# Cross-attention: value products of all four head groups in one place, partial sums in places of their own

## The chip, the cores and the metric

The kernel runs on one core of a Trainium2 chip. The metric is the device time of one execution in microseconds. The engines are TensorE (PE, with its weight loads as PEld), VectorE (DVE), ScalarE (ACT), GpSimd (POOL) and SyncE (SP), which only issues DMAs here.

## What is computed

One decoder layer on x (32 batches of 112 tokens, 512 wide): causal self-attention, cross-attention to a context of 375 tokens for each batch, and a quantised feed-forward part, each with a residual and a layer norm. The change is in the cross-attention, cut here to what matters:

```
q, k, v = hs @ Wq.T + bq, ctx @ Wk.T + bk, ctx @ Wv.T + bv     # 16 heads of 32
s      = clip(q k^T / sqrt(32), -50, 50), masked to -10000, clipped again
p      = softmax(s)                                            # over 375 tokens
ctx    = p v ; delta = rs * (ctx @ Wo.T + bo)
delta  = layernorm(delta) * gamma + beta
x      = layernorm(x + delta)
```

## The kernel before

`self_attention`, `cross_attention` and `ffn` follow each other. In `cross_attention` each engine has its own hand-written program, a loop over 32 batches b, tied to the others by semaphores. The order of the work on an engine is the order in which its `body(b, par, pair)` calls its helpers.

The 16 heads are four groups h of four heads, and the 375 context tokens are three thirds t of 125. Scores, with tokens on partitions, are 125 x 4 x 112 for one (h, t); the twelve of a batch are made in three **score blocks** of four (`score_pieces`, which splits them by group and third). Per batch:

- **TensorE** (`body`, L1293 and on): `scores` (L1286) of block 0; `attend_pair` of the batch before for head groups 2 and 3, that is two `attend` (value products, L1260, 12 matmuls each) and `sums` (L1267, column sums of the probabilities); `keys` 2 (L1206), `values` 2 (L1217); scores of block 1; keys 3; `output` of the batch before (L1238, one 128-row tile of x, into the bank `bKV[1]`); scores of block 2; `attend_pair` of this batch for groups 0 and 1; then keys 0, values 0, keys 1, values 1 of the next batch. keys write `bKV[0]`, values and output write `bKV[1]`, so each waits until the product before it in that bank was read.
- **ScalarE**: `probabilities` (L976, the exponentials of a block into `pr[h]`), copies of keys (L950) and values (L956), and `split_high` (L944), the cast of the raw context of batch b+2.
- **VectorE** (L1158 and on): `limits(b, 0)` (L1156, four instructions a block, clipping and masking), `attended(b-1, 1)`, `split_low(b+1)` (L1008, the low part of the next context, after which its raw buffer `craw` may be loaded again), `limits(b, 1)`, `tail1` (bias and statistics of the output; its first instruction, L1113, reads `bKV[1]`), `limits(b, 2)`, `attended(b, 0)`, `tail2` and `tail3` (residual, norm, row maxima). `attended(b, p)` normalises one pair of groups: a reciprocal of the sums (L1046), a product (L1048), the high parts (L1030) and low parts (L1036) into the output's operand `cT`. `cT` holds 256 columns, so 12 of the 32 batches wrap round in it and need two pieces, which doubles the instructions of L1030 and L1036.
- **GpSimd**: for each group two adds over the thirds, L920 into `psum01` and L924 into `psum`, so that `sums` has one product in place of three; between them `x1_beta` (L904) and two reciprocal roots (L908, L912). An add for a group waits until its three thirds are through `limits`.
- **SP** loads `craw` for batch b+2 (L872) once `split_low(b+1)` is done, the queries of b+1 and the x tile, and stores results.

`tile_of(b)` maps a batch to its output tile; for b = 0, 8, 16, 24 there is none, since 8 batches make 7 tiles. So the batches 1, 9, 17 and 25 have no output product and no tail; `third_value(b)` gives them another order, keys 2 ahead of the attend_pair and values 2 behind keys 3. They are called short batches, the other 26 between batch 1 and batch 31 common ones. `values` for t == 0 waits (`dl_ok`) until tail1's L1113 has read the bank:

```
if t == 0:
    wait(pe, clo_ok, b)
    wait(pe, dl_ok, tiles_done(b - 2))
```

Of the kernel before, what the change touches and what calls it, by code (L numbers as in the profile page):

```python
# [9 lines left out]
ALU = mybir.AluOpType  # L10
# [4 lines left out]
B, S, D = 32, 112, 512  # L15
T = 375
TP = 376
P = 128
C = D // P
# [731 lines left out]
def cross_attention(nc, ctxT, maskT, craw, w, bk, bv, bo, ln_gamma, ln_beta, rscale, x1_d, q_d, x2_d, x2_first, amax):  # L751
# [6 lines left out]
    with ExitStack() as ctx:  # L758
# [5 lines left out]
        bot, gam, bet = n.sb("bo", [P, D]), n.sb("gam", [P, D]), n.sb("bet", [P, D])  # L764
# [12 lines left out]
        psum01, psum = n.sb("psum01", [TW, NJ, S]), n.sb("psum", [TW, NJ, 2 * S])  # L777
        spare = LEFT["qb"][:].rearrange("p b c s -> p (b c s)")
        one, at, rinv = spare[0:1, D:D + P], spare[:, D + P:D + P + 2 * S], spare[:, D + P + 2 * S:D + P + 4 * S]
        CR = 2  # L780
# [66 lines left out]
        def _(sp):  # L847
# [15 lines left out]
            for t, src in ((bot, row(bo, P)), (gam, row(ln_gamma, P)), (bet, row(ln_beta, P))):  # L863
                sp.dma_start(t[:], src).then_inc(small_in, 16)
            sp.wait_ge(x1_out, 16 * NG)
            sp.dma_start(wraw_o[:], xwo).then_inc(wo_in, 16)
            sp.wait_ge(q_out, 16 * (NG + 1))

# [20 lines left out]
        def _(pool):  # L889
# [10 lines left out]
            def x1_beta(t):  # L900
# [3 lines left out]
                nc.gpsimd.tensor_tensor(x1[t % 2][:], x1[t % 2][:], bet[:], ALU.add).then_inc(x1b_ok, 1)  # L904
# [9 lines left out]
            def body(b, par, pair):  # L914
                tail = tile_of(b - 1)
                for h in range(C):
                    if not (last(b) and h >= 2):
                        pool.wait_ge(pr_ok, 12 * b + 3 * h + 3)
                        wait(pool, ps_ok, 4 * b + h)
                        nc.gpsimd.tensor_tensor(psum01[:], third(h, 0), third(h, 1), ALU.add).then_inc(p01_ok, 1)  # L920
                        pool.wait_ge(p01_ok, 4 * b + h + 1)
                        if h % 2 == 0:
                            wait(pool, sum_done, 2 * b + h // 2)
                        nc.gpsimd.tensor_tensor(psum[:, :, value_columns(h)], psum01[:], third(h, 2), ALU.add).then_inc(ps_ok, 1)  # L924
# [80 lines left out]
        def _(dve):  # L1005
# [152 lines left out]
            def body(b, par, pair):  # L1158
                tail = tile_of(b - 1)
                limits(b, 0)  # L1160
                if not first(b):
                    attended(b - 1, 1)
# [12 lines left out]
                attended(b, 0)  # L1175
# [25 lines left out]
        def _(pe):  # L1201
            def keys(b, par, m):
                wait(pe, k_ok, 4 * b + m)
                for c in range(C):
# [59 lines left out]
            def sums(b, p):  # L1264
                pe.wait_ge(ps_ok, 4 * b + 2 * p + 2)
                for j in range(NJ):
                    mm = nc.tensor.matmul(bPV[p][j * HD:(j + 1) * HD, 2 * S:4 * S], ones[0:TW, :], psum[:, j, :], start=True, stop=True)  # L1267
# [22 lines left out]
            def attend_pair(b, par, p):  # L1290
                for h in (2 * p, 2 * p + 1):
                    attend(b, par, h)
                sums(b, p)  # L1293

            def body(b, par, pair):
# [3 lines left out]
                if not first(b):  # L1299
                    attend_pair(b - 1, 1 - par, 1)  # L1300
# [10 lines left out]
                attend_pair(b, par, 0)  # L1311
                if not last(b):
# [534 lines left out]
```

## Time and profile before

| | |
|---|---|
| three runs | 1435.27, 1436.67, 1438.06 us; median 1436.67 |
| the profiled execution | 1435.54 us, its span 1433.7 us |
| busy, share of the span | PE 98%, PEld 78%, DVE 75%, ACT 48%, POOL 38% |
| POOL L920, 126 adds | 166.2 us, 1319 ns each; idle before them 288.0 us, waiting for DVE L1156 |
| DVE L1156, 384 limits | 221.6 us, 635 ns each |
| DVE L1046, 63 reciprocals | 97.5 us, 1548 ns each |
| PE L1260, 3072 records | 87.6 us |
| PE L1267, 504 records | 35.4 us |
| ctxT into wraw, 32 loads | 752 KB each, 4.9 us to landing |

The cross-attention runs from about 355 to 1213 us of the span. Busy time alone does not bound it: a matmul's record contains its drain, which the next one overlaps, so the distance between starts is what a stage costs TensorE. Idle time of an engine counts only where another waits for what it then does. In the profile's timelines a row merges neighbours of one kind: start, length, engine, line, operands, count, and in brackets the idle time before it and what ended that.

### The profile page before, as it was taken

The numbers are of one execution on the slowest core, as the hardware profiler recorded it, in microseconds if no ns is written. First come the engines' busy times: TensorE is split into PE (matmuls) and PEld (weight loads), VectorE is DVE, ScalarE is ACT, GpSimd is POOL, SyncE is SP. The second block draws the span as 40 slices with busy tenths as digits, with TensorE's granted clock in tenths as the row PEclk, the third lists the DMA queues.
The fourth block names the chain that finished last, engine by engine and source line by source line (L and its number), as shares of the span: only waits on it lengthen the run. The fifth ranks groups of instructions, "written<-read, shape, count | busy, mean of one in ns | idle before, by whom it ended". The sixth has DMA issues, their size and how long they took to land. (4 is left out here: it accounts for less than half of the span.)

```text
span 1433.7 us, 30674 instructions
## 1 busy us (share of the span) xinstructions
PE 1400.7 (98%) x12827; PEld 1116.9 (78%) x12836; DVE 1080.2 (75%) x2010; ACT 685.9 (48%) x995; POOL 545.1 (38%) x499
## 2 busy tenths in 40 slices
PE   8999999999999999999999999999999996999998
PEld 4889898987888888888888888888888885555443
DVE  5888676654568878777787778878768877677898
ACT  2444444442443343443343434434433434888996
POOL 1000000000345444454554444544444542752676
PEclk9999999999999999999999999999999998999999
DMA  6536424232321121121211211211212121338896
GB/s 227 166 100 166 141 97 134 101 113 104 109 73 44 51 80 43 45 72 52 66 57 51 72 37 51 80 47 50 71 45 79 44 63 48 104 134 321 279 342 208
DMA packets 93882, 149.34 MB, mean 104 GB/s; under 512 B 14002, under 2 KB 61746, under 8 KB 91954
## 3 DMA queue, kind: packets, MB, share of 16 engines
q1 hardware_dynamic: 93746, 147.41, 31.3%
q8 instruction: 100, 1.64, 0.5%
q14 instruction: 36, 0.29, 0.1%
HBM read 101.25 MB, written 44.04 MB: 101 GB/s over the span
## 5 line engine op out<-in xcount | busy, mean ns | idle before, releaser
L1156 DVE TENSOR_SCALAR xa_pr<-xa_pr,xa_keep 125x448 f32<-125x448 f32 x384 | 221.6, 635 | 92.0 <-ACT xa_pr L976 91.4
L920 POOL TENSOR_TENSOR xa_psum<-xa_pr 125x448 f32<-125x448 f32 x126 | 166.2, 1319 | 288.0 <-DVE xa_pr L1156 287.0
L976 ACT ACTIVATE xa_pr<-xa_bSC 125x1344 f32<-125x1344 f32 (+2 forms) x192 | 165.7, 916 | 131.2 <-PE xa_bSC L1286 131.2
L956 ACT COPY xa_v<-xa_bKV 125x512 f32<-125x512 f32 x96 | 56.3, 587 | 215.1 <-PE xa_bKV L1217 209.6
L924 POOL TENSOR_TENSOR xa_psum<-xa_psum,xa_pr 125x448 f32<-125x448 f32 x126 | 147.7, 1172 | 10.2 <-PE xa_bPV L1267 0.7
L1206 PE MATMUL xa_bKV<-left_xn,wA 128*128 128x376 f32 x768 | 148.3, 341 | 0.0
L1206 PE MATMUL xa_bKV<-xa_cx,wA 128*128 128x376 f32 x768 | 147.5, 341 | 0.0
L950 ACT ACTIVATE xa_kf<-xa_bKV,xa_bk 128x376 f32<-128x376 f32 x128 | 73.7, 576 | 150.2 <-PE xa_bKV L1206 150.0
L1217 PE MATMUL xa_bKV<-wZ,left_xn 128*125 128x512 f32 x576 | 141.8, 394 | 1.9 <-POOL xa_ones L891 1.9
L1206 PEld LDWEIGHTS xa_bKV<-left_xn,wA 128*128 128x128 f32 x768 | 131.2, 188 | 14.2 <-issue 10.7
L1206 PEld LDWEIGHTS xa_bKV<-xa_cx,wA 128*128 128x128 f32 x768 | 130.2, 188 | 13.7 <-issue 10.0
L1217 PE MATMUL xa_bKV<-wZ,xa_cx 128*125 128x512 f32 x576 | 140.8, 393 | 0.0
L1217 PEld LDWEIGHTS xa_bKV<-wZ,left_xn 128*125 128x125 f32 x576 | 106.0, 185 | 25.2 <-POOL xa_ones L891 2.3
L1217 PEld LDWEIGHTS xa_bKV<-wZ,xa_cx 128*125 128x125 f32 x576 | 106.0, 185 | 21.8
L1286 PEld LDWEIGHTS xa_bSC<-xa_qf,xa_kf 32*125 32x125 f32 x3072 | 92.4, 183 | 36.4 <-issue 35.4
L1286 PE MATMUL xa_bSC<-xa_qf,xa_kf 32*125 32x112 f32 x3072 | 109.4, 279 | 1.4 <-ACT xa_kf L950 1.4
L1766 PE MATMUL ff_bF<-w2q,ff_hq 128*128 128x512 bf16 x439 | 98.1, 384 | 3.6 <-DVE ff_hq L1664 2.1
L1046 DVE RECIPROCAL left_qb<-xa_bPV 128x224 f32<-128x224 f32 x63 | 97.5, 1548 | 4.2 <-PE xa_bPV L1267 4.2
L1743 PE MATMUL ff_bF<-ff_xqT,w1q 128*128 128x448 bf16 x512 | 99.9, 357 | 0.2 <-DVE ff_xqT L1640 0.2
L1766 PEld LDWEIGHTS ff_bF<-w2q,ff_hq 128*128 128x128 bf16 x448 | 44.1, 99 | 57.3 <-issue 4.9
L1260 PE MATMUL xa_bPV<-xa_pr,xa_v 125*32 125x112 f32 x3072 | 87.6, 262 | 0.4 <-DVE xa_pr L1156 0.4
L1743 PEld LDWEIGHTS ff_bF<-ff_xqT,w1q 128*128 128x128 bf16 x512 | 50.1, 99 | 47.0 <-issue 1.7
(252 smaller groups left out, 2413.5 us busy)
## 6 DMA issues: line engine op xcount, KB each, us to landing
wraw<-in_ctxT SPq DMA_DIRECT2D x32, 752.0 KB, 4.9
ff_hr<-h_scratch SPq DMA_DIRECT2D x28, 512.0 KB, 6.3
wraw<-in_w SPq DMA_DIRECT2D x7, 1024.0 KB, 5.1
xa_qf<-q_scratch SPq DMA_DIRECT2D x32, 224.0 KB, 4.9
xa_x<-x_scratch SPq DMA_DIRECT2D x28, 256.0 KB, 4.9
x_scratch<-xa_x SPq DMA_DIRECT2D x28, 256.0 KB, 2.0
h_scratch<-ff_hq SPq DMA_DIRECT2D x8, 896.0 KB, 4.9
h_scratch<-ff_hs SPq DMA_DIRECT2D x8, 896.0 KB, 4.4
```

Source lines behind the costliest of these rows:

```text
L920: nc.gpsimd.tensor_tensor(psum01[:], third(h, 0), third(h, 1), ALU.add).then_inc(p01_ok, 1)
L924: nc.gpsimd.tensor_tensor(psum[:, :, value_columns(h)], psum01[:], third(h, 2), ALU.add).then_inc(ps_ok, 1)
L950: nc.scalar.activation(kf[:, m, :], bKV[0][:, 0:TP], ACT.Identity, bias=bkt[:, m:m + 1]).then_inc(k_ok, 1)
L976: nc.scalar.activation(pr[h][:, :, t * S:(t + size) * S], bSC[0:TW, :, slot * S:(slot + size) * S], ACT.Exp, scale=XSCALE).then_inc(exp_ok, 1)
L1046: nc.vector.reciprocal(rinv, bank[:, 2 * S:4 * S]).then_inc(ri_ok, 1)
L1156: nc.vector.tensor_scalar(third(h, t), third(h, t), EM50, keep[:, b * TC + t:b * TC + t + 1], ALU.max, ALU.min).then_inc(pr_ok, 1)
L1206: mm = nc.tensor.matmul(bKV[0][:, 0:TP], w["k"][l][:, c, m * P:(m + 1) * P], cx[par][r][:, c, :], start=c == 0 and k == 0, stop=c == C - 1 ...
L1217: mm = nc.tensor.matmul(bKV[1][0:TW, 0:D], cx[par][l][:, c, t * TW:(t + 1) * TW], w["v"][r][:, c, :], start=c == 0 and k == 0, stop=c == C ...
L1260: mm = nc.tensor.matmul(bank[j * HD:(j + 1) * HD, value_columns(h)], v[par][:, t, h * P + j * HD:h * P + (j + 1) * HD], pr[h][:, j, t * S: ...
L1286: mm = nc.tensor.matmul(bSC[0:TW, j, i * S:(i + 1) * S], kf[own, h, t * TW:(t + 1) * TW], qf[par][own, h, :], start=True, stop=True)
L1743: mm = nc.tensor.matmul(bF[m % 4][:, 0:GT], w1q[:, c, m * P:(m + 1) * P], xqT[par][:, c, :], start=c == 0, stop=c == C - 1)
L1766: mm = nc.tensor.matmul(bF[(UT * u + j) % 8][:, 0:D], hq[:, u % 2, m, j * P:(j + 1) * P], w2q[:, m, :], start=m == 0, stop=m == M - 1)
```

## The change

`attend_pairs` replaces `attend_pair`: behind score block 0 of batch b TensorE now makes the value products of all four head groups of batch b-1 and then both sum groups. None are left behind score block 2, but in the last batch, whose first two groups stay there. VectorE's `attended(b-1, 0)` and `attended(b-1, 1)` both come first in its batch. GpSimd's partial sums of a batch have four places of their own in a `psum` twice as wide; `psum01` goes, the second add is made in place, and the first waits for the sums of the batch before. `bet` (ln_beta) moves into a spare part of another buffer to make room, so it is loaded later. `keys` for m == 0 waits for `clo_ok` itself.

```
-        bot, gam, bet = n.sb("bo", [P, D]), n.sb("gam", [P, D]), n.sb("bet", [P, D])
+        bot, gam = n.sb("bo", [P, D]), n.sb("gam", [P, D])
...
-        psum01, psum = n.sb("psum01", [TW, NJ, S]), n.sb("psum", [TW, NJ, 2 * S])
+        psum = n.sb("psum", [TW, NJ, C * S])
...
+        bet = spare[:, D + P + 4 * S:2 * D + P + 4 * S]
...
             sp.wait_ge(q_out, 16 * (NG + 1))
+            sp.dma_start(bet, row(ln_beta, P)).then_inc(small_in, 16)
...
                         pool.wait_ge(pr_ok, 12 * b + 3 * h + 3)
-                        wait(pool, ps_ok, 4 * b + h)
-                        nc.gpsimd.tensor_tensor(psum01[:], third(h, 0), third(h, 1), ALU.add).then_inc(p01_ok, 1)
+                        own = psum[:, :, h * S:(h + 1) * S]
+                        wait(pool, sum_done, 2 * b + h // 2 - 1)
+                        nc.gpsimd.tensor_tensor(own, third(h, 0), third(h, 1), ALU.add).then_inc(p01_ok, 1)
                         pool.wait_ge(p01_ok, 4 * b + h + 1)
-                        if h % 2 == 0:
-                            wait(pool, sum_done, 2 * b + h // 2)
-                        nc.gpsimd.tensor_tensor(psum[:, :, value_columns(h)], psum01[:], third(h, 2), ALU.add).then_inc(ps_ok, 1)
+                        nc.gpsimd.tensor_tensor(own, own, third(h, 2), ALU.add).then_inc(ps_ok, 1)
...
                 tail = tile_of(b - 1)
+                if not first(b):
+                    attended(b - 1, 0)
+                    attended(b - 1, 1)
                 limits(b, 0)
-                if not first(b):
-                    attended(b - 1, 1)
...
-                attended(b, 0)
+                if last(b):
+                    attended(b, 0)
...
                 wait(pe, k_ok, 4 * b + m)
+                if m == 0:
+                    wait(pe, clo_ok, b)
...
-            def attend_pair(b, par, p):
-                for h in (2 * p, 2 * p + 1):
-                    attend(b, par, h)
-                sums(b, p)
+            def attend_pairs(b, par, pairs):
+                for p in pairs:
+                    attend(b, par, 2 * p)
+                    attend(b, par, 2 * p + 1)
+                for p in pairs:
+                    sums(b, p)
...
                 if not first(b):
-                    attend_pair(b - 1, 1 - par, 1)
+                    attend_pairs(b - 1, 1 - par, range(2))
...
                 scores(b, par, 2)
-                attend_pair(b, par, 0)
-                if not last(b):
+                if last(b):
+                    attend_pairs(b, par, range(1))
+                else:
                     for t in range(2):
                         keys(b + 1, 1 - par, t)
                         values(b + 1, 1 - par, t)
```

TensorE, one common batch, from its first score block (L1286, after the change L1291) to the next batch's keys. `xa_bSC` are scores, `xa_bPV` value products and sums, `xa_bKV` keys, values and output. Before:

```order
L1286 MATMUL xa_bSC<-xa_qf,xa_kf 125x112 x16
L1260 MATMUL xa_bPV<-xa_pr,xa_v 32x112 x24
L1267 MATMUL xa_bPV<-xa_psum,xa_ones 32x224 x4
L1206 MATMUL xa_bKV<-xa_cx,wA 128x376 x12
L1217 MATMUL xa_bKV<-wZ,xa_cx 125x512 x12
L1286 MATMUL xa_bSC<-xa_qf,xa_kf 125x112 x16
L1206 MATMUL xa_bKV<-xa_cx,wA 128x376 x12
L1238 MATMUL xa_bKV<-wQ,xa_cT 128x512 x12
L1286 MATMUL xa_bSC<-xa_qf,xa_kf 125x112 x16
L1260 MATMUL xa_bPV<-xa_pr,xa_v 32x112 x24
L1267 MATMUL xa_bPV<-xa_psum,xa_ones 32x224 x4
L1206 MATMUL xa_bKV<-left_xn,wA 128x376 x12
```

and after the change:

```order
L1291 MATMUL xa_bSC<-xa_qf,xa_kf 125x112 x16
L1265 MATMUL xa_bPV<-xa_pr,xa_v 32x112 x48
L1272 MATMUL xa_bPV<-xa_psum,xa_ones 32x224 x8
L1211 MATMUL xa_bKV<-xa_cx,wA 128x376 x12
L1222 MATMUL xa_bKV<-wZ,xa_cx 125x512 x12
L1291 MATMUL xa_bSC<-xa_qf,xa_kf 125x112 x16
L1211 MATMUL xa_bKV<-xa_cx,wA 128x376 x12
L1243 MATMUL xa_bKV<-wQ,xa_cT 128x512 x12
L1291 MATMUL xa_bSC<-xa_qf,xa_kf 125x112 x16
L1211 MATMUL xa_bKV<-left_xn,wA 128x376 x12
```

The rows of 24 value products and 4 sums behind the third score block are gone, and those behind the first have doubled.

VectorE, one common batch in which the batch before is not cut in pieces, from its first instruction behind the tail before to the first of tail1 (L1113, then L1114). `left_qb` holds the reciprocals and products, `xa_cT` is the output's operand. Before:

```order
L1156 TENSOR_SCALAR xa_pr<-xa_pr,xa_keep 125x4x112 x4
L1046 RECIPROCAL left_qb<-xa_bPV 128x224
L1048 TENSOR_TENSOR left_qb<-xa_bPV,left_qb 128x224
L1030 TENSOR_SCALAR xa_cT<-left_qb,xa_bv 128x112 x2
L1036 SCALAR_TENSOR_TENSOR xa_cT<-left_qb,xa_bv,xa_cT 128x112 x2
L1008 TENSOR_TENSOR xa_cx<-wraw,xa_cx 128x1504
L1156 TENSOR_SCALAR xa_pr<-xa_pr,xa_keep 125x4x112 x4
L1113 TENSOR_TENSOR left_qb<-xa_bKV,xa_bo 128x512
```

and after the change:

```order
L1047 RECIPROCAL left_qb<-xa_bPV 128x224
L1049 TENSOR_TENSOR left_qb<-xa_bPV,left_qb 128x224
L1031 TENSOR_SCALAR xa_cT<-left_qb,xa_bv 128x112 x2
L1037 SCALAR_TENSOR_TENSOR xa_cT<-left_qb,xa_bv,xa_cT 128x112 x2
L1047 RECIPROCAL left_qb<-xa_bPV 128x224
L1049 TENSOR_TENSOR left_qb<-xa_bPV,left_qb 128x224
L1031 TENSOR_SCALAR xa_cT<-left_qb,xa_bv 128x112 x2
L1037 SCALAR_TENSOR_TENSOR xa_cT<-left_qb,xa_bv,xa_cT 128x112 x2
L1157 TENSOR_SCALAR xa_pr<-xa_pr,xa_keep 125x4x112 x4
L1009 TENSOR_TENSOR xa_cx<-wraw,xa_cx 128x1504
L1157 TENSOR_SCALAR xa_pr<-xa_pr,xa_keep 125x4x112 x4
L1114 TENSOR_TENSOR left_qb<-xa_bKV,xa_bo 128x512
```

A second reciprocal with its product and parts has come in, and both now stand ahead of the first four limits, and so ahead of L1008 (L1009), split_low, and of all that follows it.

## Rows read from the trace of the kernel before

**Rows 1.** Timeline, PE, one common batch (start us, us, engine, line, operation, count)

```profile
702.98 1.14 PE L1286 MATMUL xa_bSC<-xa_qf,xa_kf 32*125 32x112 f32 x32
704.04 1.36 PE L1260 MATMUL xa_bPV<-xa_pr,xa_v 125*32 125x112 f32 x48
...
717.90 1.36 PE L1260 MATMUL xa_bPV<-xa_pr,xa_v 125*32 125x112 f32 x48
719.07 0.56 PE L1267 MATMUL xa_bPV<-xa_psum,xa_ones 125*32 125x224 f32 x8
719.56 2.35 PE L1206 MATMUL xa_bKV<-left_xn,wA 128*128 128x376 f32 x12
721.75 2.96 PE L1217 MATMUL xa_bKV<-wZ,left_xn 128*125 128x512 f32 x12
...
729.49 1.14 PE L1286 MATMUL xa_bSC<-xa_qf,xa_kf 32*125 32x112 f32 x32
```

**Rows 2.** Timeline, PE, batch 1, a short one

```profile
389.86 1.14 PE L1286 MATMUL xa_bSC<-xa_qf,xa_kf 32*125 32x112 f32 x32
...
393.18 1.36 PE L1260 MATMUL xa_bPV<-xa_pr,xa_v 125*32 125x112 f32 x48
...
403.84 2.35 PE L1206 MATMUL xa_bKV<-left_xn,wA 128*128 128x376 f32 x12
...
413.77 1.14 PE L1286 MATMUL xa_bSC<-xa_qf,xa_kf 32*125 32x112 f32 x32
```

**Rows 3.** Timeline, DVE, normalising a pair: whole, then parts of one in pieces

```profile
394.99 1.56 DVE L1046 RECIPROCAL left_qb<-xa_bPV 128x224 f32<-128x224 f32 x1 [1.05 <-PE xa_bPV L1267]
...
397.01 0.47 DVE L1030 TENSOR_SCALAR xa_cT<-left_qb,xa_bv 128x112 fp32r<-128x112 f32 x2
...
397.88 1.72 DVE L1008 TENSOR_TENSOR left_xn<-wraw,left_xn 128x1504 fp32r<-128x1504 f32 x1
...
724.86 0.99 DVE L1030 TENSOR_SCALAR xa_cT<-left_qb,xa_bv 128x80 fp32r<-128x80 f32 x4
...
725.77 0.83 DVE L1036 SCALAR_TENSOR_TENSOR xa_cT<-left_qb,xa_bv,xa_cT 128x80 fp32r<-128x80 f32 x4
```

**Rows 4.** Timeline, DVE and POOL, limits, split_low and adds, batch 0 and a common one

```profile
369.55 1.54 DVE L1156 TENSOR_SCALAR xa_pr<-xa_pr,xa_keep 125x448 f32<-125x448 f32 x4 [7.91 <-ACT xa_pr L976]
...
370.81 2.91 POOL L920 TENSOR_TENSOR xa_psum<-xa_pr 125x448 f32<-125x448 f32 x1 [10.94 <-DVE xa_pr L1156]
371.01 1.72 DVE L1008 TENSOR_TENSOR xa_cx<-wraw,xa_cx 128x1504 fp32r<-128x1504 f32 x1
...
711.03 1.71 DVE L1008 TENSOR_TENSOR left_xn<-wraw,left_xn 128x1504 fp32r<-128x1504 f32 x1
...
716.94 0.69 DVE L1113 TENSOR_TENSOR left_qb<-xa_bKV,xa_bo 128x512 f32<-128x512 f32 x1 [1.51 <-PE xa_bKV L1238]
...
719.51 3.34 DVE L1156 TENSOR_SCALAR xa_pr<-xa_pr,xa_keep 125x448 f32<-125x448 f32 x4
...
720.03 1.30 POOL L920 TENSOR_TENSOR xa_psum<-xa_pr 125x448 f32<-125x448 f32 x1
```

**Rows 5.** Groups of instructions by line (busy us, mean ns of one, idle before)

```profile
L924 POOL TENSOR_TENSOR xa_psum<-xa_psum,xa_pr 125x448 f32<-125x448 f32 x126 | 147.7, 1172 | 10.2 <-PE xa_bPV L1267 0.7
...
L950 ACT ACTIVATE xa_kf<-xa_bKV,xa_bk 128x376 f32<-128x376 f32 x128 | 73.7, 576 | 150.2 <-PE xa_bKV L1206 150.0
...
L904 POOL TENSOR_TENSOR xa_x<-xa_x,xa_bet 128x512 f32<-128x512 f32 x28 | 36.2, 1293 | 0.0
```

**Rows 6.** Timeline, SP's queue and ACT, batch 1: the raw context and its cast

```profile
399.62 0.55 SPq L872 DMA_DIRECT2D wraw<-in_ctxT  x1
...
404.52 1.45 ACT L944 CAST xa_cx<-wraw 128x1504 fp32r<-128x1504 f32 x1 [0.65 <-DMA wraw<-in_ctxT]
```

**Rows 7.** Timeline, PE, last batch, value products of group 2

```profile
1191.95 0.78 PE L1260 MATMUL xa_bPV<-xa_pr,xa_v 125*32 125x112 f32 x24 [0.38 <-DVE xa_pr L1156]
```

**Rows 8.** Stretches: us, PE, PEld, DVE, ACT, POOL busy, PEclk, DMA share, GB/s

```profile
1198.00:1199.00 1.00, 1.00 (x11) 0.43 (x13) 0.74 (x3) 0.00 (x0) 0.00 (x0) 0.57 0.00 0
```

More of the change, by code:

```diff
@@ L862, in _ @@
             sp.dma_start(craw, ctxT[1]).then_inc(c_in, 16)
-            for t, src in ((bot, row(bo, P)), (gam, row(ln_gamma, P)), (bet, row(ln_beta, P))):
+            for t, src in ((bot, row(bo, P)), (gam, row(ln_gamma, P))):
                 sp.dma_start(t[:], src).then_inc(small_in, 16)
@@ L903, in x1_beta @@
                 pool.wait_ge(x1_in[t % 2], 16 * (t // 2) + 16)
-                nc.gpsimd.tensor_tensor(x1[t % 2][:], x1[t % 2][:], bet[:], ALU.add).then_inc(x1b_ok, 1)
+                nc.gpsimd.tensor_tensor(x1[t % 2][:], x1[t % 2][:], bet, ALU.add).then_inc(x1b_ok, 1)
             def norm(t):
@@ L1266, in sums @@
                 for j in range(NJ):
-                    mm = nc.tensor.matmul(bPV[p][j * HD:(j + 1) * HD, 2 * S:4 * S], ones[0:TW, :], psum[:, j, :], start=True, stop=True)
+                    mm = nc.tensor.matmul(bPV[p][j * HD:(j + 1) * HD, 2 * S:4 * S], ones[0:TW, :], psum[:, j, 2 * p * S:2 * (p + 1) * S], start=True, stop=True)
                 mm.then_inc(sum_done, 1)
```

## The prediction

> **What bounds the kernel now.** I read the table of waits first: from batch 1 on TensorE hardly waits in the whole stage, so I went to its order of time and looked at one batch as a sum of stages. In [rows 1] a common batch runs from its first score block at 702.98 to the next at 729.49, 26.51 us, with each stage beginning where the last one ends. The other kind, batches 1, 9, 17 and 25, has no output product; batch 1 takes from 389.86 to 413.77, 23.91 us [rows 2]. Of the 31 steps from one batch to the next, 26 are common, 4 are short, and one is batch 0's. So TensorE is the bound in this stage, and VectorE, ScalarE and GpSimd run behind it. Then I read VectorE's order of time beside GpSimd's, since the change reorders VectorE's work. VectorE is busy for most of a batch, so it has no large reserve, and what matters is which of its results TensorE waits for, and when.
>
> **What TensorE saves.** The value products and sums behind score block 2 go. In [rows 1] they hold TensorE from 717.90 to 719.56, 1.66 us. In the first place 24 value products and 4 sums are added to equal ones. Products run from 717.90 to 719.07, 1.17 us for 24 with the change of shape; the added 24 I put at 1.10. A sum group holds 0.49 (719.07 to 719.56); the added one at 0.38, near the 0.35 of the shortest possible overlap of its two passes (the group's own record is 0.56 long, most of it drain). Both ends: 1.45 and 1.66. So TensorE gains 0.18 a batch, between 0 and 0.21. That is all the change can give there: at most 31 x 0.18 = 5.6 us. Batch 0 has no pair from before it, so it loses the whole 1.66.
>
> **What VectorE now delays.** Times below count from the start of a batch's first score block. Formerly VectorE began a batch with the limits of block 0, normalised one pair behind them (the second pair of the batch before), and the other pair at the batch's end, behind all limits. Now both pairs of the batch before come first. They can't begin until the sums are there: score block 1.06 (702.98 to 704.04), the extra products 1.10, and from the first product to the reciprocal 1.81 (393.18 to 394.99) [rows 1 to 3]: 3.97. One pair takes 2.89 (394.99 to 397.88) [rows 3], two take 5.78, to 9.75. Limits of block 0: 1.46 (369.55 to 371.01) [rows 4], to **11.2**. Only then comes split_low, which began at 8.05 before (711.03 - 702.98); there follow the limits of block 1 and tail1, whose first instruction frees the bank in which TensorE puts the next batch's first value product.
>
> Limits and GpSimd's sums get in each other's way. Four limits take 1.54 alone and 3.34 when two adds run beside them, and the add that began at 370.81, just before split_low, took 2.91, while split_low took its usual 1.72 [rows 4]. So the two engines exclude each other, instruction by instruction. In the changed order GpSimd gets the first head's probabilities at 11, and its two adds, x1_beta and the next head's first add all fall on the limits of block 1, where formerly the first two had already run beside the reciprocal. With L920 1.30 [rows 4], L924 1.17 and L904 1.29 [rows 5]: split_low 1.72; the blocked add ends 2.71 behind split_low's start (371.01 to 373.72); then 1.17 + 1.29 + 1.30, small gaps of 0.1, and 0.25 for the last limit: 6.8 from 11.2, so **18.0**. The read of the output bank (L1113) adds 0.69 [rows 4]: 18.7, 18.75 with the signal.
>
> The Trainium skill (SBUF — State Buffer, "Who interferes with whom") says that a VectorE instruction with two SBUF inputs and a reading GpSimd instruction exclude each other and that issue order decides who blocks. By that rule split_low, issued 0.2 behind the add, would wait for it, about 0.9 us that the row of batch 0 does not show; the sum below would be 3.6 us longer, over four short batches.
>
> **Common batches.** TensorE could begin the value product at 721.75 - 702.98 - 0.18 = 18.6. It waits for 18.75 and, its weights no longer loaded ahead, loses 0.1 more; from there 7.74 (721.75 to 729.49) [rows 1]: 26.6. Against 26.51 that is **+0.1**. In 12 of the 26 the batch before is cut into two pieces by the 256-column buffer, and each pair has eight small instructions in place of four: 0.99 + 0.83 [rows 3] against 0.47 and the rest to 397.88, 0.87 together. The difference is at most 0.95, but the first of the four had to wait for an add. I take 0.5 a pair: **+1.1** a batch (bounds +0.6 and +1.9).
>
> **Short batches.** TensorE's products begin at 3.32 (389.86 to 393.18) [rows 2], so VectorE is 2.26 later: split_low begins at 13.5 and is done at 15.2. TensorE reaches the next batch's keys at 403.84 - 389.86 = 13.98, less 0.17 (a wait for a sum that goes), less 0.18: 13.6. It waits **1.6**. split_low also frees the raw context for its transfer: 4.90 from issue to the cast (399.62 to 404.52), cast 1.45 [rows 6], the copy of the keys 0.58 [rows 5]: 22.2, where TensorE wants the second key product at 15.2 + 4.97 = 20.2 (one keys and one values product, half of 719.56 to 729.49 [rows 1]). It waits **2.0** more. Then 4.97 to the end: 27.2 against 23.91, **+3.3**, four times. In common batches the transfer lands at 11.2 + 1.7 + 4.9 = 17.8, and score block 2 ends only at 16.4 (717.90 - 702.98 + 1.48), with its exponentials ahead of the cast: nothing.
>
> **The end.** In the last batch TensorE waits for the limits of block 2 already, 0.38 [rows 7]. They start at 16.53 in a common batch (719.51 - 702.98); now at 11.2 + 5.2 (limits of block 1 with the same four GpSimd instructions, without split_low) + 2.57 of tail1 (716.94 to 719.51) = 19.0 [rows 4]. I take **+2.3**, between 1.5 and 3. The load of ln_beta moves on SP's queue behind the waits for x1_out and q_out, ahead of the first wait for split_low; it is first used in batch 2, so nothing. GpSimd's own adds keep their number and size (in place and strided: the second add was strided before, and 1.17), nothing.
>
> **Sum.** 14 x 0.1 + 12 x 1.1 + 4 x 3.3 - 1.7 + 2.3 = 1.4 + 13.2 + 13.2 + 0.6 = **+28.4**. The profiled execution took 1435.5 us around a span of 1433.7; that gives 1463.9. The median of the three runs is 1.1 above it: **1465**.
>
> **Rivals.** (A) Limits and adds interleave better than I have it: VectorE passes its four limits of block 1 before GpSimd's second add, so they end near 11.2 + 1.7 + 1.5 = 14.4 and tail1's read waits only for the output product, as before. For it speaks 369.55 to 371.01, four limits and split_low without a delay, against it 3.34 for four. Then common batches gain 0.18 and only the short ones and the ends lose: -4.7 + 13.2 + 0.6 = +9, **1446**. (B) They interleave worse, or a pair costs 3.4 (the split ones 4): a microsecond more in each of 26 batches, **1491**; for it speaks that the order of the two engines is a matter of tenths. (C) The clock. After TensorE's pause at the end of the stage the granted clock fell from 1.0 to 0.5, 0.57 in the microsecond at 1198 [rows 8], which is 1.2 in place of 2.4 GHz; the pause before it was 2.5 us. If each short batch's two pauses (1.6 and 2.0) did the same for 3.4 us, 1.7 us lost each time, it is 7 to 14 more: **1475**. (D) On the other side, faster: VectorE's chain is short enough everywhere, TensorE keeps its 0.18 in all batches and the short ones don't wait: -5.6 and -1.7, **1430**. It needs split_low done by 13.6 in the short batches, so pairs of at most 2.1 us, where a reciprocal alone is 1.56 [rows 3] and the product and four other instructions follow; and a transfer of under 3 us. I see no room for it.
>
> **How the numbers follow.** Forecast 0.56, A 0.16, B 0.12, C 0.11, D 0.05. The forecast's own bounds are 1457 to 1479 (the cut batches 7 to 23 in place of 13, the short ones 12 to 17, the end 1.5 to 3). The range takes in A and C and leaves out B and D: **1445 to 1485**. About 0.2% (2.9 us) is what a measurement here tells from no change. Faster 0.04, within it 0.02, slower 0.94.
>
> **What would show it.** Right: TensorE waits at its values line for VectorE's L1114 in common batches, about 0.2 and 1.3 us by turns, at the keys line for split_low and for ScalarE's key copy in batches 1, 9, 17 and 25, near 2 us each; score blocks 26.6 and 27.6 apart by turns, and 27.2 in the short ones; reciprocals start 4.0 behind the batch. Wrong: waits of TensorE only in the short batches (A), or over 2 us in common ones (B), a granted clock of 0.5 within the stage (C), batches 26.3 apart (D).

## The result, and the profile after

The changed kernel takes **1472.53 us**, the median of four runs (1471.5 to 1477.62), against 1436.18 for the kernel before on the same chip: a ratio of **1.0258, 95% interval 1.0246 to 1.027** (here and below estimated from the single runs, so not quite the quotient of the two medians). It is slower by 36 us. The profiled execution took 1471.5 us around a span of 1469.7, 36.0 more than the 1433.7 of before, so its trace can be read against the sum of the prediction as it stands.

The page's groups for the limits (L1157), the first and the second add of a head (L923, L925), and from the view by lines the add of ln_beta to x1 (L906):

```profile
L923 POOL TENSOR_TENSOR xa_psum<-xa_pr 125x448 f32<-125x448 f32 x126 | 210.0, 1667 | 378.3 <-DVE xa_pr L1157 377.4
L1157 DVE TENSOR_SCALAR xa_pr<-xa_pr,xa_keep 125x448 f32<-125x448 f32 x384 | 319.6, 894 | 10.6 <-ACT xa_pr L977 10.5
...
L925 POOL TENSOR_TENSOR xa_psum<-xa_psum,xa_pr 125x448 f32<-125x448 f32 x126 | 157.1, 1247 | 9.9
...
L906 POOL TENSOR_TENSOR xa_x<-xa_x,left_qb 128x512 f32<-128x512 f32 x28 | 40.0, 1427 | 0.0
```

The same 384 limits, on the same data, took 98 us more than before (319.6 against 221.6, that is 384 x 635 ns, on the page of before). The adds are longer too: the first took 1319 ns before, the second 1172 ns [rows 5]. No work was added to either engine; they stand in each other's way more often. What TensorE makes of it stands in its table of waits (total in us, times, longest):

```profile
PE xa_bKV L1222 <- DVE left_qb L1114: 15.5, 17, 1.5
PE xa_bKV L1211 <- DVE left_xn L1009: 6.8, 4, 1.7
PE xa_bKV L1211 <- ACT xa_kf L951: 6.4, 4, 2.3
```

None of the three was there before. The first is the read of the output bank, in common batches; the other two are split_low and the key copy, once each in the four short batches. Here is TensorE's order of time in one common batch whose pairs are cut in pieces:

```profile
741.78 1.14 PE L1291 MATMUL xa_bSC<-xa_qf,xa_kf 32*125 32x112 f32 x32
742.85 2.51 PE L1265 MATMUL xa_bPV<-xa_pr,xa_v 125*32 125x112 f32 x96
745.17 0.94 PE L1272 MATMUL xa_bPV<-xa_psum,xa_ones 125*32 125x224 f32 x16
746.04 2.35 PE L1211 MATMUL xa_bKV<-left_xn,wA 128*128 128x376 f32 x12
...
758.29 2.32 PE L1211 MATMUL xa_bKV<-xa_cx,wA 128*128 128x376 f32 x12
761.77 3.02 PE L1222 MATMUL xa_bKV<-wZ,xa_cx 128*125 128x512 f32 x12 [1.16 <-DVE left_qb L1114]
...
769.56 0.70 PE L1291 MATMUL xa_bSC<-xa_qf,xa_kf 32*125 32x112 f32 x16
```

and VectorE's and GpSimd's in the same batch:

```profile
745.80 1.56 DVE L1047 RECIPROCAL left_qb<-xa_bPV 128x224 f32<-128x224 f32 x1 [1.82 <-PE xa_bPV L1272]
...
749.28 1.55 DVE L1047 RECIPROCAL left_qb<-xa_bPV 128x224 f32<-128x224 f32 x1
...
752.68 1.54 DVE L1157 TENSOR_SCALAR xa_pr<-xa_pr,xa_keep 125x448 f32<-125x448 f32 x4
754.13 1.72 DVE L1009 TENSOR_TENSOR xa_cx<-wraw,xa_cx 128x1504 fp32r<-128x1504 f32 x1
755.77 5.26 DVE L1157 TENSOR_SCALAR xa_pr<-xa_pr,xa_keep 125x448 f32<-125x448 f32 x4
760.95 0.68 DVE L1114 TENSOR_TENSOR left_qb<-xa_bKV,xa_bo 128x512 f32<-128x512 f32 x1
...
753.93 2.93 POOL L923 TENSOR_TENSOR xa_psum<-xa_pr 125x448 f32<-125x448 f32 x1 [11.25 <-DVE xa_pr L1157]
756.95 1.17 POOL L925 TENSOR_TENSOR xa_psum<-xa_psum,xa_pr 125x448 f32<-125x448 f32 x1
758.07 1.44 POOL L906 TENSOR_TENSOR xa_x<-xa_x,left_qb 128x512 f32<-128x512 f32 x1
759.47 1.31 POOL L923 TENSOR_TENSOR xa_psum<-xa_pr 125x448 f32<-125x448 f32 x1
```

Read it as a chain. Value products for all four head groups and their sums stand between the score block and the next keys, which follow 4.26 us behind its start; the reciprocal begins at 4.02. Two pairs, in pieces here, take 3.48 and 3.40. Then come the limits of block 0, split_low, and four limits that take 5.26 us in place of 1.54, because each has one of GpSimd's four adds in its way. (GpSimd's first, L923, is the one that had begun before split_low.) L1114, which frees the output bank, starts 19.17 behind the batch. TensorE stood ready at 760.6 and waits 1.16 us. In the kernel before, the same read waited 1.51 us for TensorE, not the other way round [rows 4].

The two waits of a short batch, batch 1, by VectorE, TensorE and ScalarE:

```profile
401.31 1.72 DVE L1009 TENSOR_TENSOR left_xn<-wraw,left_xn 128x1504 fp32r<-128x1504 f32 x1
...
403.18 2.32 PE L1211 MATMUL xa_bKV<-left_xn,wA 128*128 128x376 f32 x12 [1.69 <-DVE left_xn L1009]
...
407.80 1.45 ACT L945 CAST xa_cx<-wraw 128x1504 fp32r<-128x1504 f32 x1 [4.51 <-DMA wraw<-in_ctxT]
409.15 0.57 ACT L951 ACTIVATE xa_kf<-xa_bKV,xa_bk 128x376 f32<-128x376 f32 x1
...
409.77 2.33 PE L1211 MATMUL xa_bKV<-left_xn,wA 128*128 128x376 f32 x12 [1.48 <-ACT xa_kf L951]
...
414.81 1.14 PE L1291 MATMUL xa_bSC<-xa_qf,xa_kf 32*125 32x112 f32 x32
```

Distances from score block to score block, read from TensorE's order of time over the whole stage, for both kernels and the eight experiments (us):

| kernel | batch 0 | short (1, 9, 17, 25) | common, not cut / cut | first to last score block |
|---|---|---|---|---|
| before | 22.83 | 23.91, 23.91, 23.75, 23.75 | 26.51 to 26.54 / the same | 807.89 |
| changed | 21.16 | 27.08, 27.07, 28.33, 27.92 | 26.70 to 26.79 / 27.79 to 28.13 | 840.26 |
| places alone | 22.84 | 23.89 to 23.91 | 26.51 to 26.54 / the same | 808.20 |
| VectorE's order alone | 22.84 | 29.46, 29.40, 26.78, 28.31 | 26.51 to 26.54 / the same | 826.53 |
| split_low first | 21.18 | 23.61 | 26.36 to 26.39 / the same | 801.47 |
| ln_beta's add later | 21.18 | 27.25, 27.22, 28.13, 28.01 | 26.36 to 26.39 / 26.75 to 27.13 | 822.81 |
| split_low first in short batches | 21.16 | 23.61 | 26.70 to 26.79 / 27.79 to 28.14 | 824.47 |
| limits and split_low first | 21.17 | 23.61 | 27.36 to 27.59 / 28.43 to 30.05 | 853.08 |
| split_low first, last batch | 21.17 | 23.61 | 26.36 to 26.39 / the same | 801.46 |
| before, split_low first | 22.83 | 23.75 | 26.51 to 26.54 / the same | 807.56 |

### The profile page after: what moved, and what is told of

The parts are those of the page before. It is cut to its first block and busy times, and to the rows that moved or that the text cites. A ratio compares the mean times of both kernels' runs of the same rounds, so it can differ in the third digit from the quotient of the medians.

```text
span 1469.7 us, 30639 instructions
## 1 busy us (share of the span) xinstructions
PE 1404.3 (96%) x12827; PEld 1118.9 (76%) x12836; DVE 1161.1 (79%) x2010; ACT 683.4 (46%) x995; POOL 599.0 (41%) x499
## 5 line engine op out<-in xcount | busy, mean ns | idle before, releaser
L923 POOL TENSOR_TENSOR xa_psum<-xa_pr 125x448 f32<-125x448 f32 x126 | 210.0, 1667 | 378.3 <-DVE xa_pr L1157 377.4
L1157 DVE TENSOR_SCALAR xa_pr<-xa_pr,xa_keep 125x448 f32<-125x448 f32 x384 | 319.6, 894 | 10.6 <-ACT xa_pr L977 10.5
L1211 PE MATMUL xa_bKV<-left_xn,wA 128*128 128x376 f32 x768 | 150.1, 344 | 13.2 <-DVE left_xn L1009 6.8
L925 POOL TENSOR_TENSOR xa_psum<-xa_psum,xa_pr 125x448 f32<-125x448 f32 x126 | 157.1, 1247 | 9.9
L1222 PE MATMUL xa_bKV<-wZ,left_xn 128*125 128x512 f32 x576 | 142.7, 396 | 10.7 <-DVE left_qb L1114 8.4
L1222 PE MATMUL xa_bKV<-wZ,xa_cx 128*125 128x512 f32 x576 | 142.2, 395 | 8.2 <-DVE left_qb L1114 7.0
L1222 PEld LDWEIGHTS xa_bKV<-wZ,left_xn 128*125 128x125 f32 x576 | 105.3, 185 | 37.2 <-issue 11.6
L1222 PEld LDWEIGHTS xa_bKV<-wZ,xa_cx 128*125 128x125 f32 x576 | 105.1, 185 | 34.4 <-issue 12.4
L1291 PEld LDWEIGHTS xa_bSC<-xa_qf,xa_kf 32*125 32x125 f32 x3072 | 92.4, 183 | 36.4 <-issue 34.0
L1291 PE MATMUL xa_bSC<-xa_qf,xa_kf 32*125 32x112 f32 x3072 | 109.5, 279 | 1.4 <-ACT xa_kf L951 1.4
L1243 PE MATMUL xa_bKV<-wQ,xa_cT 128*128 128x512 f32 x336 | 83.9, 398 | 3.6 <-DVE xa_cT L1037 3.6
```

Of the source, the lines that this page charges most:

```text
L923: nc.gpsimd.tensor_tensor(own, third(h, 0), third(h, 1), ALU.add).then_inc(p01_ok, 1)
L925: nc.gpsimd.tensor_tensor(own, own, third(h, 2), ALU.add).then_inc(ps_ok, 1)
L1157: nc.vector.tensor_scalar(third(h, t), third(h, t), EM50, keep[:, b * TC + t:b * TC + t + 1], ALU.max, ALU.min).then_inc(pr_ok, 1)
L1211: mm = nc.tensor.matmul(bKV[0][:, 0:TP], w["k"][l][:, c, m * P:(m + 1) * P], cx[par][r][:, c, :], start=c == 0 and k == 0, stop=c == C - 1 ...
L1222: mm = nc.tensor.matmul(bKV[1][0:TW, 0:D], cx[par][l][:, c, t * TW:(t + 1) * TW], w["v"][r][:, c, :], start=c == 0 and k == 0, stop=c == C ...
L1243: mm = nc.tensor.matmul(bKV[1][:, 0:D], cT[l][:, c, own], w["o"][r][:, c, :], start=c == 0 and k == 0 and not last(b), stop=c == C - 1 and ...
```

## The experiments

The first four ran on one chip beside 20 runs of the kernel before (median 1435.94), the last four on another beside 15 (median 1436.73). Line numbers of an experiment are its own and may be one to three off.

### Places alone

```diff
 # the changed kernel, with TensorE's and VectorE's order as before
-                if not first(b):
-                    attended(b - 1, 0)
-                    attended(b - 1, 1)
                 limits(b, 0)
+                if not first(b):
+                    attended(b - 1, 1)
...
-                if last(b):
-                    attended(b, 0)
+                attended(b, 0)
...
-                    attend_pairs(b - 1, 1 - par, range(2))
+                    attend_pairs(b - 1, 1 - par, range(1, 2))
...
-                if last(b):
-                    attend_pairs(b, par, range(1))
-                else:
+                attend_pairs(b, par, range(1))
+                if not last(b):
```

> The changed kernel with TensorE's and VectorE's order put back as before: only the four places for the partial sums, the second add in place, ln_beta loaded later and the wait for clo_ok at keys stay. My theory (the loss is VectorE's order): no difference from before, 1436 us, between 1433 and 1439. Rival (GpSimd's in-place, strided adds or the waits on sum_done cost something): L923 or L925 longer than 1.32 and 1.17 us a piece on average, and up to 10 us slower.

Measured: 1436.85, ratio 1.0002 (0.9993 to 1.0011). The first add took 1323 ns and the second, now in place and with another stride, 1171 ns on its page, against 1172 before [rows 5]. So the wider partial sums, the adds in place, the later load of ln_beta and the wait for split_low at the first key product cost nothing that can be measured. All of the loss is in the order of TensorE's and VectorE's work.

### VectorE's order alone

```diff
 # the kernel before
-                limits(b, 0)
                 if not first(b):
+                    attended(b - 1, 0)
                     attended(b - 1, 1)
+                limits(b, 0)
...
-                attended(b, 0)
+                if last(b):
+                    attended(b, 0)
```

> The kernel before, with VectorE's order alone changed: attended(b-1, 0) and attended(b-1, 1) ahead of limits(b, 0); TensorE's order untouched. My theory: the first pair's sums are ready when the batch begins, so VectorE starts it some 3 us earlier than in the changed kernel, tail1's read is in time in common batches (26.5 us each as before), and only the four short batches lose, near 3.2 us each, for split_low and the key copy: 1436 + 13 = 1449 us, 1445 to 1453. Rival (the order alone carries the whole loss, whatever TensorE does): 1470.

Measured: 1454.55, ratio 1.0123 (1.0108 to 1.0139), 5 us above the expected value and over its upper end of 1453. TensorE makes its products as before, so VectorE finds one pair's sums ready at the end of the batch before, and its chain is a pair shorter than in the changed kernel: the common batches lose nothing at all (26.51 to 26.54). Only the four short ones lose, 3.0 to 5.6 us each. In batch 1, TensorE's timeline and one stretch (us, busy time of PE, PEld, DVE, ACT, POOL, then PEclk, DMA share, GB/s):

```profile
402.75 0.78 PE L1262 MATMUL xa_bPV<-xa_pr,xa_v 125*32 125x112 f32 x24 [0.81 <-DVE xa_pr L1156]
405.34 0.97 PE L1269 MATMUL xa_bPV<-xa_psum,xa_ones 125*32 125x224 f32 x8 [1.80 <-POOL xa_psum L924]
406.24 4.13 PE L1208 MATMUL xa_bKV<-left_xn,wA 128*128 128x376 f32 x12
...
406.00:408.00 2.00, 2.00 (x10) 1.76 (x7) 2.00 (x2) 0.53 (x1) 1.92 (x2) 0.50 0.03 8
```

The waits are 0.81 for limits and 1.80 for a sum, 2.6 in all, in each of the four batches. In batch 1 the granted clock fell during the second of them to 0.50, the lower of TensorE's two levels, 1.2 GHz, and stayed there for nearly 7 us; twelve key products took 4.13 us in place of 2.3. That is what the expectation lacked in size: batch 17, at full clock, cost 3.0; batches 1 and 9, where it fell for 7 us, 5.6 and 5.5; batch 25, where it fell for 3.4, 4.6. The expectation also had the wrong waits: it named split_low and the key copy, and this kernel's table of waits has neither. TensorE waits for the limits of block 1 and for the GpSimd adds behind them, because it still wants the first pair's products and sums at the end of the same batch. So the 3.2 a batch that it expected was near the 3.0 at full clock by luck, and what this run shows is that VectorE's order costs the common batches nothing without the gathered products. It does not show the loss of the changed kernel's short batches on its own.

### split_low first

```diff
 # the changed kernel
+                if not last(b):
+                    split_low(b + 1, 1 - par)
                 if not first(b):
                     attended(b - 1, 0)
                     attended(b - 1, 1)
                 limits(b, 0)
-                if not last(b):
-                    split_low(b + 1, 1 - par)
                 limits(b, 1)
```

> The changed kernel with one thing moved: VectorE makes split_low(b+1) ahead of both attended, in the time in which it waits for the sums. My theory: split_low leaves the chain between the sums and tail1's read (1.7 us of it, and the add it blocks), the short batches wait for neither split_low nor the transfer, so all batches run at TensorE's pace, 26.3 and 23.6 to 23.7 us, and only the end keeps 2.7: 1436 - 6 - 1.7 + 2.7 = 1431 us, 1428 to 1437, faster than both. Rival (what delays is the two pairs themselves, 5.8 us ahead of the limits): 14 x 0.25 + 12 x 1.3 stay, 1455.

Measured: **1433.06, ratio 0.9979 (0.9969 to 0.9988)**: faster than both kernels, by moving one instruction of 1.72 us. VectorE and TensorE in a common batch whose score block starts at 697.76:

```profile
699.43 1.72 DVE L1009 TENSOR_TENSOR left_xn<-wraw,left_xn 128x1504 fp32r<-128x1504 f32 x1
701.78 1.56 DVE L1047 RECIPROCAL left_qb<-xa_bPV 128x224 f32<-128x224 f32 x1 [0.63 <-PE xa_bPV L1272]
...
707.63 6.71 DVE L1157 TENSOR_SCALAR xa_pr<-xa_pr,xa_keep 125x448 f32<-125x448 f32 x8
714.26 0.68 DVE L1114 TENSOR_TENSOR left_qb<-xa_bKV,xa_bo 128x512 f32<-128x512 f32 x1
...
716.38 2.96 PE L1222 MATMUL xa_bKV<-wZ,left_xn 128*125 128x512 f32 x12
```

split_low runs where VectorE had nothing to do, before the sums are there. The limits still collide with GpSimd (eight in 6.71, where two times 1.54 is 3.1), but L1114 ends at 714.94, 1.4 ahead of TensorE's need. All waits that the change had brought into the stage are gone, and a common batch takes 0.15 less than before. That is the saving of TensorE that the prediction put at 0.18, seen here without anything on top of it. What the move brought depends on the batch: the bank's read starts 16.5 us behind the batch in place of 18.15 where the pairs are whole, the length of split_low earlier, but at 15.5 in place of 19.16 where they are cut, twice that.

### ln_beta's add later

```diff
 # the changed kernel, GpSimd
-                    if h == 0 and tail is not None:
-                        x1_beta(tail)
                     if h == 1 and tail is not None:
                         norm(tail)
+                        x1_beta(tail)
```

> The changed kernel with one thing moved on GpSimd: x1_beta (one add of 128x512, 1.29 us) behind the root of tail1 instead of between the adds of head groups 0 and 1, so that the limits of block 1 meet three GpSimd instructions in place of four. My theory (VectorE's limits wait for each GpSimd add in turn): limits of block 1 take 3.9 in place of 5.26 us, common batches 26.4 and 26.6 in place of 26.8 and 27.8, short ones unchanged at 27 to 28: 1472.5 - 14 x 0.35 - 12 x 1.2 = 1453 us, 1449 to 1459. Rival (the limits are slow there for another reason, the adds only beside them): unchanged, 1472.

Measured: 1454.11, ratio 1.0125 (1.0109 to 1.014). The limits of block 1 and the bank's read, in a cut batch:

```profile
696.36 4.23 DVE L1156 TENSOR_SCALAR xa_pr<-xa_pr,xa_keep 125x448 f32<-125x448 f32 x4
700.50 0.68 DVE L1113 TENSOR_TENSOR left_qb<-xa_bKV,xa_bo 128x512 f32<-128x512 f32 x1
...
701.33 3.02 PE L1221 MATMUL xa_bKV<-wZ,xa_cx 128*125 128x512 f32 x12
```

4.23 in place of 5.26: one add of GpSimd less beside the four limits makes them 1.03 us shorter, and that reaches TensorE whole: cut batches fall from 27.8 to 26.8, and the others, which had only 0.4 to give, to 26.4, where TensorE alone sets them. The short batches, which have no such add, stay at 27.2 to 28.1. The clock fell to 0.50 for 3.4 us in two of them, 9 and 25, right behind the wait for split_low: batch 9 took 27.22, and batch 1, where it did not fall, 27.25.

### split_low first in the short batches alone

```diff
 # the changed kernel
+                if not last(b) and tail is None:
+                    split_low(b + 1, 1 - par)
                 if not first(b):
                     attended(b - 1, 0)
                     attended(b - 1, 1)
                 limits(b, 0)
-                if not last(b):
+                if not last(b) and tail is not None:
                     split_low(b + 1, 1 - par)
```

> The changed kernel with split_low(b + 1) ahead of both pairs in the batches without an output product alone (0, 1, 9, 17, 25). My theory: the short batches lose because split_low comes late, the common ones because the limits of block 1 and with them the read of the output bank come late; the two are separate. Then the short batches go from 27.1 to 28.3 us down to about 23.7 (15 us of the stage come back), and the common ones stay at 26.7 and 27.8: 1457 us, between 1453 and 1460. Rival: the delay is passed on from batch to batch, so that the common ones that follow a short one lose less too: under 1450. Other rival: the short batches wait for the transfer or the reads of GpSimd and stay above 26: over 1464.

Measured: 1456.4, ratio 1.0132 (1.0116 to 1.0147). The short batches are at 23.61, the common ones unchanged. The stage is 15.8 us shorter than in the changed kernel. So the two losses are separate, and neither is handed on to the next batch.

### Limits and split_low first

```diff
 # the changed kernel
-                if not first(b):
-                    attended(b - 1, 0)
-                    attended(b - 1, 1)
                 limits(b, 0)
                 if not last(b):
                     split_low(b + 1, 1 - par)
+                if not first(b):
+                    attended(b - 1, 0)
+                    attended(b - 1, 1)
                 limits(b, 1)
```

> The changed kernel with the limits of block 0 and split_low ahead of both pairs. The number of VectorE's instructions is that of the fast version that has split_low alone first. Theory: VectorE's order matters by when the low parts of the second pair and the read of the output bank are ready; with limits (from 2.5 us on, since they wait for exponentials) and split_low first, the pairs begin near 5.7 in place of 4, end near 11.5, and TensorE's output product and everything behind it wait. Common batches 27.4 and by turns 28.4, 1462 to 1480 us, 1470 likely. Rival: what hurts is only how the limits of block 0 and 1 fall together with GpSimd's adds behind the pairs; then limits of block 0 first are harmless and this is as fast as split_low alone first, 1430 to 1437 us.

Measured: 1482.25, ratio 1.0321 (1.0304 to 1.0338), the slowest of all, and 2 above the end of what was expected. The common batches are where they were expected, 27.4, and four of the twelve cut ones too, 28.4; the other eight took 30.0. Two cut batches, and a stretch of the first:

```profile
453.92 4.61 PE L1243 MATMUL xa_bKV<-wQ,xa_cT 128*128 128x512 f32 x12 [1.85 <-DVE xa_cT L1037]
...
511.33 3.03 PE L1243 MATMUL xa_bKV<-wQ,xa_cT 128*128 128x512 f32 x12 [1.84 <-DVE xa_cT L1037]
...
455.00:457.00 2.00, 2.00 (x6) 1.61 (x5) 0.32 (x1) 0.00 (x0) 1.92 (x2) 0.50 0.00 0
```

The wait is the same, the output product that follows is not: 3.03 at full clock, 4.61 at half. Eight times 1.57 (30.02 against 28.45) is 12.6 us, and without them this kernel would be at 1470, the value expected. What makes this order bad is that TensorE now waits for the pairs' low parts (L1037): they end about 14.4 us behind the batch's start (453.8 - 439.4), where they end near 10.9 in a cut batch with split_low alone first (707.63 - 697.76, and 1.0 for the pieces).

### The last batch

```diff
 # the version with split_low first
                 if not last(b):
                     split_low(b + 1, 1 - par)
+                else:
+                    limits(b, 0)
                 if not first(b):
                     attended(b - 1, 0)
                     attended(b - 1, 1)
-                limits(b, 0)
+                if not last(b):
+                    limits(b, 0)
```

> The fast version (split_low alone ahead of both pairs) with the last batch's limits of block 0 ahead of its two pairs, where VectorE otherwise waits 2.1 us for the sums. Theory: in the last batch TensorE waits for the limits of block 2 (1.3 us); these come 1.5 us earlier or more, so 1 to 2 us are gained: 1431.5 us, between 1430 and 1433. Rival: the wait only moves on to the pair that TensorE asks for next, and the time stays at 1433.

Measured: **1431.95, ratio 0.9962 (0.9948 to 0.9975)**. TensorE's wait for the limits of block 2 went back from 1.32 to what it was before [rows 7]:

```profile
1186.80 0.78 PE L1268 MATMUL xa_bPV<-xa_pr,xa_v 125*32 125x112 f32 x24 [0.38 <-DVE xa_pr L1157]
```

From the last batch's first score block to amax (the reduction of the row maxima behind it) it is 40.94 us against 41.66, a gain of 0.7 where 1 to 2 were expected; the intervals of the two versions overlap, so the whole times don't tell them apart. It is the best version of the study by its median, 4.8 below the kernel before.

### The kernel before with split_low first

```diff
 # the kernel before
+                if not last(b):
+                    split_low(b + 1, 1 - par)
                 limits(b, 0)
                 if not first(b):
                     attended(b - 1, 1)
-                if not last(b):
-                    split_low(b + 1, 1 - par)
```

> The kernel before, with split_low(b + 1) ahead of the limits of block 0. Theory: before, TensorE waits for nothing in the common batches, so where split_low stands changes nothing there; the 3 us of the fast version come from the value products in one place (0.15 us a batch). 1436 us, between 1434.5 and 1438. Rival: the 3 us come from split_low's early place, and are had without the change: 1432 to 1434.

Measured: 1436.73, ratio 0.9999 (0.999 to 1.0008), nothing. The gain of the two fast versions is therefore the change's own: value products in one place are worth 0.15 us a common batch (3.9 in all) and 0.1 to 0.3 a short one, once VectorE's order is fit for them. The 1.67 of batch 0 is no such gain. The pair that batch 0 no longer makes is made in the last batch, whose next keys follow 4.26 us behind its start in place of 2.74; from that start to amax it was 38.37 us before and is 41.66 and 40.94 in the two fast versions. That is how a stage that is 6.4 us shorter leaves 3 to 5 us of the whole time.

## Why the prediction was right, and where its sizes were off

The direction, the mechanism and each of the places were right: 1465 was forecast, between 1445 and 1485, and 1472.5 was measured. Against the profiled execution the sum reads, in us over the whole kernel:

| term | predicted | measured |
|---|---|---|
| batch 0 | -1.7 | -1.7 |
| 14 common, not cut | +1.4 | +3.3 |
| 12 common, cut | +13.2 | +15.7 |
| 4 short | +13.2 | +15.1 |
| last batch to amax | +2.3 | +2.7 |
| before the first and behind amax | 0 | +0.9 |
| sum | +28.4 | +36.0 |

**TensorE's saving.** 0.18 a batch was predicted; 0.15 was seen wherever nothing waits (26.51 to 26.36).

**The chain of VectorE, step by step.** The reciprocal came at 4.02 (3.97 predicted). Whole pairs took 2.97 and 2.88 (2.89 each), and the limits of block 0 began at 9.87 in a batch after an uncut one (9.75). From there split_low and the limits of block 1 beside four GpSimd instructions took as long as worked out: the output bank's read began at 18.15 (18.0). The value product followed at 18.97 (18.75). The wait's own error is thus made of 0.05, 0.07, 0.03 and 0.07 us, all in one direction, of no weight once. From the value product to the next batch it took 7.80, where the prediction had 7.74 and 0.1 more for weights not loaded ahead, which gives back 0.04. But a common batch lost 0.24 and not 0.1, and a cut one 1.3 and not 1.1, and 26 times that is 4.4 us of the 7.6 by which the sum was short. The step that was mis-sized is **"18.7, 18.75 with the signal"**, held against a need at 18.6. Where two numbers that nearly meet are repeated 26 times, the hundredths are the term.

**Cut batches.** The pieces added 0.51 and 0.52 to the two pairs; 0.5 a pair was taken, as half of the upper bound. A cut batch lost 1.07 more than an uncut one, where 1.0 was forecast (1.1 against 0.1), so what was missing is mostly the 0.14 to 0.20 of all common batches. Batch 3 took 28.13, with a wait of 1.54: the limits of block 0 began at 11.26 in it, against 10.90 in the other cut ones.

**Short batches.** Batch 1 has split_low at 13.58 (13.5), a first wait of 1.69 (1.6), a second of 1.48 (2.0), and a distance of 27.08 (27.2). The second wait is shorter because TensorE's product before it began at 15.44 and not at 15.2, and the key copy ended at 22.0 and not at 22.2. Batches 17 and 25 took 28.33 and 27.92, which no step had; both also took 23.75 before and not 23.91, which the prediction took for all four. In batch 17 the raw context took 5.98 us from issue to cast, not the 4.90 of [rows 6], and the clock fell:

```profile
838.41 0.55 SPq L874 DMA_DIRECT2D wraw<-in_ctxT  x1
...
838.53 3.84 PE L1211 MATMUL xa_bKV<-left_xn,wA 128*128 128x376 f32 x12 [1.69 <-DVE left_xn L1009]
...
840.00:842.00 2.00, 2.00 (x8) 2.00 (x8) 2.00 (x3) 0.00 (x0) 1.67 (x2) 0.50 0.91 302
...
844.39 1.45 ACT L945 CAST xa_cx<-wraw 128x1504 fp32r<-128x1504 f32 x1 [5.76 <-DMA wraw<-in_ctxT]
845.75 0.57 ACT L951 ACTIVATE xa_kf<-xa_bKV,xa_bk 128x376 f32<-128x376 f32 x1
...
846.37 2.35 PE L1211 MATMUL xa_bKV<-left_xn,wA 128*128 128x376 f32 x12 [1.19 <-ACT xa_kf L951]
```

That is the sign of rival C, once in four short batches and nowhere else in this stage, but not its price. The second key product waits for the key copy, the copy for the cast, and the cast for the transfer, so the slower products (3.84 in place of 2.32) only shortened TensorE's second wait, to 1.19. The 1.25 us by which batch 17 is longer than batch 1 are the transfer's: its cast began at 21.30 behind the batch, in batch 1 at 20.07. In batch 25 the clock held, the transfer took 5.57, the second wait was 2.31, and the batch was 0.84 longer. The version with ln_beta's add later has the control: there batch 9, with the clock fallen, was no longer than batch 1, and batch 17, without a fall and with a transfer of 5.77, took 28.13. Why the transfers differ is open. The one run at 1477.62 had a mean clock of 0.988 against 0.992 in the two fastest; it has no trace of its own, so whether the clock made it longer is not shown.

**The end.** Limits of block 2 of the last batch began 19.05 behind it (19.0), and TensorE waited 1.33 for them instead of 0.38. That wait is 0.95 more; 1.52 more are the second pair's products and sums at the start of the batch, which fill time in which the prediction had TensorE wait. The two together are what it took from the limits' delay of 2.5.

**Outside the stage.** 1.4 us more behind amax, 0.5 less ahead of the first score block. The code there is the same, and the stretch behind amax was between 219.8 and 222.2 us long in the ten profiled executions, without order between them: scatter, as far as the runs show, and not explained by them.

**The rivals.** A (limits pass ahead of the adds) fell: 5.26 for four. Even with the add of ln_beta taken out, the four took 4.23. B fell: no common batch lost more than 1.62, and a whole pair cost 2.9. C's sign was there once in the stage and cost nothing; it cost 1.5 to 2.5 us a time in other orders (VectorE's order alone, limits and split_low first). D, faster, was wrong for this kernel as it stands, and for the reason given, split_low too late for the short batches. But it counted without the room at the start of a batch: with split_low there the short batches don't wait, the common ones keep their saving, and the time is 1433.

**What the runs settle.** That the loss lies in VectorE's order under the gathered value products, and not in gathering them: places alone, nothing; all of the change with split_low moved, no loss. VectorE's order without the gathering loses in the short batches alone, and by other waits. That the two losses are separate: 15 us come back with split_low's place in four batches, and with it in all the rest does too. That in common batches the four GpSimd instructions beside the limits of block 1 decide: one out, 1.03 less, and 18 us of the time gone. **Left open:** which of the 1.72 us of split_low and the collisions it pushes on weighs more in common batches was not taken apart beyond the 1.6 and 3.6 us by which its move brings the bank's read forward, since split_low can't be taken out without another way to make the low parts.

## What to carry to other kernels

When work is gathered into one place for the engine that is the bound, follow the engine that must prepare and clear away for it: its chain is now one piece, and what stands last in it (here a subtraction that frees a buffer, and a read that frees a bank) is late by the whole of what moved ahead. Look first for an instruction whose inputs have long been there and put it into the gap before the gathered results arrive; one instruction of 1.72 us was worth 39 us here. And where two engines exclude each other, count how many instructions of the one fall on a string of the other, since each costs about a microsecond: four limits took 1.54 us alone, 3.34 with two adds, 4.23 with three, 5.26 with four.

## What the runs showed of the hardware that was not expected

**Who goes first.** In every one of the 31 batches GpSimd's first add (L923) was issued 0.2 us before split_low (753.93 against 754.13 above). It took 2.93 us, and split_low its undisturbed 1.72. The Trainium skill (SBUF — State Buffer, "Who interferes with whom") says that issue order decides who blocks. That the two exclude each other agrees with the trace. The order doesn't, if the starts in the profile are the order of issue: the add started while the last limit still ran (to 754.22), and the instruction that came next on VectorE went ahead of the add that was already waiting. An estimate by the page's rule: the add, 1.30 undisturbed and 0.2 ahead, would have held split_low for about 1.1 us (the prediction has 0.9). Behind split_low, limits and adds took turns one by one.

**Short pauses and the clock.** In the kernel before, the clock fell in this stage only at its end, behind a pause of 2.5 us [rows 8]. Here pauses of TensorE of 1.75 to 1.86 us in the order with limits first were followed by a stretch at 0.50 in eight of twelve cases, each costing 1.6 us, and by none in the other four; of four pauses of 1.69 in the changed kernel, one was, and two of four of 1.70 with ln_beta's add later; of the four pairs of 0.81 and 1.80 with VectorE's order alone, three; of the changed kernel's twelve between 1.14 and 1.54 ahead of the value product (L1222), none; and pauses of 2.3 and 2.5 in short batches, behind an earlier one of 1.7, were followed by none. So the same pause costs its length or nearly twice that. Its length does not tell which: among the twelve, 1.75 had a fall behind it and 1.84 none, and what does tell is not shown. Where another wait follows that does not depend on TensorE, as in the short batches of the changed kernel, the fall costs nothing.
